# One kernel, five streams: the interleaving orders of all engines exchanged for others

## What is computed

```python
xa = ln(x);  sx = concat([state[:, 1:2] - xa[:, :1], xa[:, :-1] - xa[:, 1:]])
xxx = einsum(tanh((xa + sx * maa_x) @ maa_w1), maa_w2)        # low rank 32, five times
xk, xw, xv, xr, xg = xa + sx * (maa_stack + xxx)
w = exp(-exp(time_decay + tanh(xw @ td_w1) @ td_w2))
r, k, v, g = xr @ Wr.T, xk @ Wk.T, xv @ Wv.T, silu(xg @ Wg.T)
for t in steps:                                               # s: 16 x 16 for each head
    a = k_t[:, None] * v_t[None, :];  out_t = r_t @ (u * a + s);  s = a + w_t[:, None] * s
x1 = x + groupnorm(out) * g @ Wo.T
y = x1 + sigmoid(xr2 @ Wfr.T) * (square(relu(xk2 @ Wfk.T)) @ Wfv.T)   # channel mix on ln(x1)
result = y + Wo2(softmax(Wn(inorm(y)) . Wm(inorm(ctx))) @ Wl(ctx))    # cross attention, per batch
```

## Time and profile before

| | |
|---|---|
| median of three runs | 931.6 us (928.16, 931.6, 932.55) |
| span of the profiled execution | 929.8 us |
| PE busy | 861.4 us, 93% |
| DVE busy | 681.4 us, 73% |
| POOL busy | 537.9 us, 58% |
| ACT busy | 397.8 us, 43% |
| DMA moved | 100.46 MB, mean 108 GB/s |

### The profile page before, as it was taken

How to read it: one execution, slowest core, us unless ns; L and a number is a source line. 1 busy time by engine, 2 the same in 40 slices (tenths; PEclk the granted TensorE clock), 3 DMA queues, 4 the chain that set the end, 5 groups by cost and what they waited for, 6 DMA issues and landing times.

```text
span 929.8 us, 12242 instructions
## 1 busy us (share of the span) xinstructions
PE 861.4 (93%) x4388; PEld 377.5 (41%) x4388; DVE 681.4 (73%) x875; ACT 397.8 (43%) x819; POOL 537.9 (58%) x571
## 2 busy tenths in 40 slices
PE   2799998999989998999899989999979999899998
PEld 1233433343334433334343434444334444445454
DVE  5435599799998999899879999899995434523441
ACT  3022422343245223323245453753456353846495
POOL 1001577778878699799699998888983201010100
PEclk9799999899989999999899999999999999999999
DMA  8082479552766729364655135436020312010102
GB/s 295 11 140 100 135 192 163 166 148 69 156 150 152 222 81 199 107 188 107 170 170 125 45 93 114 139 78 168 19 75 12 91 34 69 1 45 1 45 1 46
DMA packets 93951, 100.46 MB, mean 108 GB/s; under 512 B 22850, under 2 KB 64066, under 8 KB 91842
## 3 DMA queue, kind: packets, MB, share of 16 engines
q1 hardware_dynamic: 86978, 87.09, 37.8%
q10 hardware_dynamic: 6912, 12.59, 3.9%
HBM read 65.05 MB, written 33.55 MB: 106 GB/s over the span
## 4 chain that ended last, share of the span: by engine, by line
PE 62%; POOL 14%; DVE 10%; issue 4%; DMA 4%; ACT 4%; SPq 2%; ACTq 0%; POOLq 0%; DVEq 0%
PE PS L1369 44%; PE PS L1609 4%; POOL VB L756 4%; PE PS L1498 4%; POOL VB L748 3%; POOL VB L752 3%; DMA scr_v<-STG 3%; PE PS L1436 2%; PE PS L1586 2%; PE PS L1378 2%; DVE M L1079 2%; DVE VB L1195 2%; DVE VB L1076 1%; SPq L500 1%; DVE SX L1076 1%
## 5 line engine op out<-in xcount | busy, mean ns | idle before, releaser
L1369 PE MATMUL PS<-M,W 128*128 128x512 f32 x544 | 270.0, 636 | 19.8 <-DVE M L1079 11.7
L1369 PEld LDWEIGHTS PS<-M,W 128*128 128x128 f32 x544 | 102.6, 200 | 158.0 <-issue 136.5
L1195 DVE TENSOR_TENSOR_SCAN VB<-PS,VB 128x512 f32<-128x512 f32 x128 | 149.1, 1206 | 17.7 <-POOL VB L756 14.2
L748 POOL TENSOR_TENSOR VB<-KR,VB 128x1008 f32<-128x1008 f32 x64 | 129.4, 2022 | 55.3 <-PE PS L1498 51.2
L756 POOL TENSOR_TENSOR VB<-VB 128x1008 f32<-128x1008 f32 x64 | 149.8, 2341 | 3.4
L1076 DVE TENSOR_TENSOR VB<-VB,PS 128x2048 f32<-128x2048 f32 x64 | 145.9, 2279 | 1.1
L638 POOL TENSOR_SCALAR NM<-MV 128x2 f32<-128x2 f32 (+1 forms) x24 | 5.8, 243 | 230.0 <-DVE MV L1326 140.8
L752 POOL TENSOR_TENSOR VB<-WG,VB 128x1008 f32<-128x1008 f32 x64 | 128.6, 2010 | 0.0
L1369 PE MATMUL PS<-W,M 128*128 128x512 f32 x224 | 103.9, 596 | 0.0
L1344 DVE TENSOR_REDUCE SM<-PS 128x1 f32<-128x512 f32 x64 | 43.1, 686 | 53.1 <-PE PS L1609 52.4
L1498 PE MATMUL PS<-VB,HEAD 128*32 128x512 f32 x512 | 68.8, 610 | 4.0 <-DVE VB L1076 4.0
(11 more groups left out here) (179 smaller groups left out, 1296.9 us busy)
## 6 DMA issues: line engine op xcount, KB each, us to landing
VB<-scr_vs SPq DMA_DIRECT2D x64, 256.0 KB, 7.3
W<-in_w SPq DMA_DIRECT2D x8, 1024.0 KB, 10.0
scr_vs<-STG SPq DMA_DIRECT2D x64, 64.0 KB, 5.6
scr_v<-STG SPq DMA_DIRECT2D x16, 256.0 KB, 6.4
scr_w<-STG ACTq DMA_DIRECT2D x16, 256.0 KB, 4.8
scr_k<-STG ACTq DMA_DIRECT2D x16, 256.0 KB, 2.0
KR<-scr_k SPq DMA_DIRECT2D x16, 256.0 KB, 3.5
WG<-scr_w SPq DMA_DIRECT2D x16, 256.0 KB, 5.7
```

Source lines behind the costliest of these rows:

```text
L748: po.tensor_tensor(vo, KO[:, 0:N2 - 1].unsqueeze(1).to_broadcast([P, S, N2 - 1]), VB[:, 2 + s, 0, :, 1:N2], ALU.mult).then_inc(g_kv, 1)
L1195: sc = dv.tensor_tensor_scan(s_, PS[:, 5, :], b_, 0.0, ALU.mult, ALU.add)
L1369: mm = pe.matmul(o, l, r, start=i == 0, stop=i == 3)
```

## The change

The five strings are replaced by five others. Nothing else is altered: every stream still issues the same instructions with the same waits and buffers, only the places at which an engine changes from one stream to another are different. The after kernel has four lines fewer ahead of the functions, so that its L1365 is the L1369 of before, its L496 the L500, and so on. Of the diff a few lines are enough to see its form:

```diff
 ORDER_PE = (
-    "a:16 l:2 a:4 m:3 p:7 a:1 p:2 a:1 p:1 m:1 p:1 a:1 p:5 m:4 a:1 p:1 m:2 p:1 m:1 p:3 m:1 p:6 m:1 p:6 m:1 "
...
+    "a:16 l:2 a:4 m:2 p:6 m:1 p:6 m:1 p:3 m:1 p:1 m:3 p:1 a:4 m:1 p:1 m:2 p:7 m:1 p:4 m:1 p:6 m:1 p:4 a:1 "
...
 ORDER_SP = (
-    "a:20 p:1 load:1 p:7 load:1 p:12 a:1 load:5 a:1 p:1 a:3 load:2 x:1 p:1 load:1 p:2 load:1 p:2 l:1 p:2 "
...
+    "a:12 x:1 a:4 l:1 a:4 p:20 a:1 load:6 l:1 p:1 a:4 x:1 load:4 p:1 load:1 p:18 a:1 p:4 load:5 end:1 "
...
```

## The result

The changed kernel takes 969.4 us (968.33 to 972.36), the kernel before beside it 932.1 (928.16 to 933.14): ratio 1.0414, 95% interval 1.0387 to 1.0441. That is 37 us slower, where I had forecast 926.1 and a range up to 940. The profiled execution has a span of 966.6 us against 929.8, +36.8.

A forecast was written before the change was run, and what follows sets the result against it. DVE and PE were taken to bound the middle, latency the start, PE the end. Terms -2, -2, +1, 0 and -2.5 sum to -5.5 us: span 924.3, plus 1.8 gives 926.1 us; range 914 to 940.

The forecast's parts named there:

- Term 4: The middle, the 64 scan turns: DVE at 91.5% turns over the same work, 0 us, bounds -5 and +5.
- Term 1: The start on PE: v projections of quarter 0 end sooner and k's first follows sooner, -2 us, bounds -2.3 and 0.
- rival 1: No change: DVE bounds the middle and its waits eat the early gain, 929 to 932 us; chance 0.16.
- Term 2: v's stores in quarters 1 to 3: reordered loads shorten waits before k's projection, 0, -1 and -1, together -2 us.
- rival 4: Quarter 1: XN's load ahead of v's last stores delays ACT's step and PE's k by 3.5 us, 929.6; chance 0.08.
- the ring rule: SP's DMA transfers share one ring per engine, consumed in order, so XN ahead delays quarter 1's last four stores by its length.
- Term 3: DVE's mixes behind the scans, quarters 1 and 3: seven come 2 to 3 us later; PE waits one more, +1 us.
- Term 5: The end, after the last scan turn: PE regains half its 5.0 us idle, -2.5 us, bounds -5 and +7.5.
- rival 5: The last lane's chain bounds the end, which gets +5 to +7.5 us: 933.6 to 936; chance 0.09.
- Rival 3: Slower by late mixes behind the scans: PE waits seven times 1.7, 12 us, then gets half clock; 937 us, chance 0.17.

The follow-up runs named there:

- The order that I made from the old one: The kernel before with 21 two-SBUF-input DVE instructions moved behind the next scan in DVE's list: 967.3 us (1.0396); with long fills for POOL's products 937.5.

## Why the prediction was wrong

- **Term 4, the middle, is the step that failed.** I wrote "DVE at 91.5% turns over the same work. 0". The instructions are the same, their durations are not: 39.7 us more of holds. I had bounded the term by the shift of work, +-5, and taken durations from the rows as constants, though the two-input rows of before stood at 820, 860 and 961 ns beside a mean of 749 for the same size with PSUM. What I named as the sign for this term, DVE's busy share at 91 to 92%, came true (91.0%) although from the first scan turn to the last 34.9 us were added, where terms 2 to 4 together had -1: held time counts as busy, so the share says nothing. What the runs show in the term's place: DVE instructions with two inputs in SBUF held by POOL's reads, 52.1 us where before had 12.4, and worth all of the loss, since it goes when POOL does not read.
- **Term 1, -2.** Right in its place: the first v projection started at 38.51, the last v store landed at 66.1 for 69.2, and k's first projection came at 68.76, 3.1 sooner, where I had worked out 68.8 from PE's own work. But it brought POOL's first product from 103.73 to 99.50 and lost 7.8 us of DVE to it. Even with the holds at the first scan kept off it did not reach the end (ratio 1.0014, no different from 1): that part is rival 1.
- **Term 2, -2.** Small and mixed. The last v store of quarter 2 landed in 4.99 us for 7.47, yet PE idled 1.15 us before k for 0.77; in quarter 3 the wait of 2.77 went. Quarter 1's XN ahead of the stores (rival 4): ACT's step waited 3.86 us for the store against 3.24, 0.6 more and not rival 4's 3.5, and PE's k did not wait for that step but followed a mix, after a wait of 2.39 for DVE. So the ring rule was not put to a test of time.
- **Term 3, +1.** PE's waits for M at L1432 are 6.5 us in 5, where the earlier trace rows has 6.0 in 6: about right. The waits for the other mixes (L1365 for L1075) doubled from 6.0 to 12.9 us; the term did not count them.
- **Term 5, -2.5.** Measured -1.7 from the last scan turn to the end. Its sign came as named: what PE does not fill there went from 9.5 us (213.80 less 204.27) to 6.9, 2.6 less. The last lane (rival 5) cost nothing to be seen: from 905 to 960 us PE is busy throughout.
- **The sum.** -5.5 for the order as such; with POOL's reading away and its length kept it measures -8.7, with copies -3.7, with short fills -6.7. The five terms come near that kernel in sum; one by one they were not measured in it. In the real one some 46 us (37.3 + 8.7) belong into term 4, which neither it nor any rival named. Rival 3 had 937 and the right sign by another mechanism. The order that I made from the old one has 12 of its 37 us from something of that kind. The lower clock that rival 3 counted on came (0.94 for 0.98 in the middle), but with the holds; what stalls alone cost with it no run shows.

The Trainium skill has the rule that was missing (SBUF — State Buffer, Who interferes with whom): a DVE instruction with two SBUF inputs contends with a GpSimd instruction that reads SBUF, not with one that only writes it. Of the shared ports it says, there for DVE's modes that use two ports, that whoever issues first has them for the whole instruction. The traces agree with the first in both halves, and with the second for DVE behind POOL: in the changed kernel 16 of the 17 caught mixes took 1.9 to 2.8 us (the other 1.0), beside fills they take 0.747 on average, and M<-PS,EXT stands at 1.22 in every kernel. So what stands ahead of the prediction, that only semaphores make one engine wait for another, does not hold for DVE and POOL: a caught mix had begun, with all its waits behind it, and still took up to 2.8 us for 0.745.

## What to carry to other kernels

When a change moves instructions, list the pairs of engines that can hold each other, here DVE with two SBUF inputs and GpSimd reading SBUF, and count in the trace of before how many meet and how long they stand above their shortest time; the sum of durations holds only while that count holds. Look at the mean of each group against its shortest and against its like with an operand elsewhere: a mean a tenth above (820 for 745 ns here) can be a hold that a new order multiplies. A gain at a start is also a shift of who comes first.

## What the runs showed of the hardware that I had not expected

- A held DVE instruction ends a fixed time behind the POOL instruction that it met, whenever it began: 0.55 us for 512 columns (32 of the 37 caught in the changed kernel), 1.08 for shifts of 1024 (the other five). One, at 214.83 us, began 0.51 behind the start of a product of 2.44 and took 2.48. POOL's next one is stretched by 0.3 to 1.0 us: 2.44 to 2.98 and 2.65 to 3.18 where 2.00 and 2.33 are the free values (the rows of after above).
- Halving POOL's product from 1008 to 504 columns takes it, in the old order, from 2.02 to 1.12 us only, so two halves cost 0.2 more than the whole: small pieces are no cheap way round a hold.
- A fill of 1008 columns took 0.94 us, a copy 1.05, a product of two tensors 2.0: on POOL the one operand that a copy reads adds 0.1, the step to a product of two adds 0.95. Whether the second read or the multiplication does it is not shown.
